# Second norm: which engine normalises, which adds, and in what order GpSimd works

## The reference

```
xn = layernorm(x)
x  = x + linear_attention(xn) + nested_attention(xn)
```

```
q, k = elu(xn @ Wq.T + bq) + 1, elu(xn @ Wk.T + bk) + 1      # linear attention
z    = layernorm(xn) * norm_w + norm_b                       # nested attention
```

## Time and profile before

| | |
|---|---|
| median of 3 runs | 4818.39 us (4813.27 to 4819.5) |
| the profiled execution: time, span | 4783.38 us, 4781.6 us |
| second norm, from its first weight load to the next phase's first load | 2499.4 to 2800.5 us of the span |
| busy in the span: PE, DVE, ACT, POOL | 4446.1, 3305.4, 1912.6, 1037.3 us |

### The profile page before, as it was taken

The page is one execution under the profiler, slowest core; times in us unless marked ns, Lnnn a source line. Parts: engine busy times, 40 slices in busy tenths (PEclk is TensorE's granted clock), DMA queues, the critical chain, the costliest instruction groups (busy, mean ns, idle before and its releaser), DMA issues. The chain is left out here.

```text
span 4781.6 us, 154458 instructions
## 1 busy us (share of the span) xinstructions
PE 4446.1 (93%) x64527; PEld 2868.5 (60%) x64527; DVE 3305.4 (69%) x5496; ACT 1912.6 (40%) x2685; POOL 1037.3 (22%) x1042
## 2 busy tenths in 40 slices
PE   5999699999999999999987879999999999999998
PEld 3444499889889888987655634444444444444443
DVE  5899755555555555554338977878787878787877
ACT  2888311111111111111233426656565656565654
POOL 1000143344334333432007760000000000000000
PEclk9999899999999999999998969999999999999999
DMA  3544411111111111111233440000000000000000
GB/s 121 169 129 126 135 50 53 54 46 51 52 54 50 53 53 47 50 53 58 74 120 105 111 106 9 9 13 9 13 9 13 9 13 9 13 9 13 9 13 9
DMA packets 261647, 250.25 MB, mean 52 GB/s; under 512 B 51712, under 2 KB 230016, under 8 KB 260256
## 3 DMA queue, kind: packets, MB, share of 16 engines
q1 hardware_dynamic: 240528, 209.39, 14.6%
q0 software_dynamic: 6144, 16.79, 1.1%
q10 hardware_dynamic: 14352, 14.55, 0.9%
HBM read 135.27 MB, written 105.38 MB: 50 GB/s over the span
## 5 line engine op out<-in xcount | busy, mean ns | idle before, releaser
L2201 DVE TENSOR_REDUCE part_max<-p_m 128x1 f32<-128x512 f32 x2118 | 1363.2, 685 | 380.8 <-PE p_m L2043 373.3
L2183 ACT ACTIVATE prob<-p_s 128x1024 f32<-128x1024 f32 x1024 | 1047.6, 1023 | 751.0 <-PE p_s L2107 748.9
L2062 PE MATMUL p_o<-prob,v_one 128*64 128x512 f32 x4096 | 1055.1, 593 | 5.2 <-ACT prob L2183 1.8
L2043 PE MATMUL p_m<-keys,queries 96*64 96x512 f16 x4236 | 661.4, 387 | 28.0 <-DMA keys<-parts_d 20.4
L2107 PE MATMUL p_s<-queries,keys 97*64 97x512 f16 x4096 | 618.9, 380 | 0.0
L2107 PEld LDWEIGHTS p_s<-queries,keys 97*64 97x64 f16 x4096 | 228.1, 109 | 599.3 <-issue 593.8
L2043 PEld LDWEIGHTS p_m<-keys,queries 96*64 96x64 f16 x4236 | 238.6, 108 | 311.2 <-DVE part_max L2201 56.4
L2011 POOL TENSOR_TENSOR attn<-o_num,o_inv 32x512 f32<-32x512 f32 x64 | 81.0, 1266 | 1459.5 <-DVE o_inv L2220 1453.1
L833 PE MATMUL pd_pre<-inv,step 64*64 64x64 f32 x10240 | 374.4, 219 | 17.9 <-issue 15.4
L2062 PEld LDWEIGHTS p_o<-prob,v_one 128*64 128x64 f32 x4096 | 287.5, 136 | 164.3 <-issue 15.8
L833 PEld LDWEIGHTS pd_pre<-inv,step 64*64 64x64 f32 x10240 | 342.7, 135 | 46.0 <-issue 45.7
(11 more groups left out here) (245 smaller groups left out, 6701.5 us busy)
## 6 DMA issues: line engine op xcount, KB each, us to landing
q_d<-conv_q SPq DMA_DIRECT2D x16, 1024.0 KB, 5.1
v_d<-conv_v SPq DMA_DIRECT2D x16, 1024.0 KB, 5.1
k_d<-conv_k SPq DMA_DIRECT2D x16, 1024.0 KB, 6.5
sums<-sums_d SPq DMA_DIRECT2D x128, 128.0 KB, 2.9
k_t<-k_d SPq DMA_DIRECT2D x32, 512.0 KB, 4.6
q_t<-q_d SPq DMA_DIRECT2D x32, 512.0 KB, 3.4
v_t<-v_d SPq DMA_DIRECT2D x32, 512.0 KB, 3.3
slots_d<-zero ACTq DMA_DIRECT2D x1, 10112.0 KB, 31.2
```

The source lines that it names most:

```text
L2043: last = te.matmul(p_m[k % 2][x * HALF:(x + 1) * HALF, :], queries[0:ROW, p, hh, at:at + HALF], keys[0:ROW, 2 * p + hh, kb * BLK:(kb + 1) ...
L2062: product = te.matmul(p_o[64 * hh:64 * hh + VW, :], g.v_one[:, j, p, hh:hh + 2, :].rearrange("p a d -> p (a d)"), prob[:, j % 2, hh, :], s ...
L2183: a.activation(prob[:, j % 2], p_s[j % 2][:], ACT.Exp, scale=SCORE_SCALE).then_inc(exp_d, 1)
L2201: v.tensor_reduce(part_max[:, hh * SUB + sub, kb:kb + 1], p_m[k % 2][:], AX.X, ALU.max).then_inc(red_d, 1)
```

## The change

Four things change, all in `phase_second_norm`. Both normalisations go from VectorE to ScalarE, as an activation `Identity` with scale `rstd` and bias `shift`, which GpSimd's `root` makes as -mean * rstd in one more instruction. `add_base` and `query_features` go from GpSimd to VectorE. GpSimd's step becomes `root(a, 0)`, `fetch(s + 1)`, `root(a, 1)`, `remainders(d)`. ScalarE's step becomes `normed(a)`, `key_exp(c)`, `low(d)`, `query_exp(c)`, `keep_turned(b)`, `nested(a)`, `high(c)`; VectorE's becomes `residual(a)`, `sums(d)`, `keys_values(c)`, `normed(a)` (the statistics alone), `queries(c)`, `add_base(a)`, `values(c)`, `query_features(c)`.

```diff
+    shift = sb("s_shift", [P, 2, 2])
...
-        def root(a, n, mv_d, ve_d, rs_d, used_d):
+        def root(a, n, mv_d, ve_d, rs_d, sh_d, used_d):
...
             po.tensor_tensor(rstd[:, r, n:n + 1], var_eps[:, r, n:n + 1], g.minus_half[:], ALU.pow).then_inc(rs_d, 1)
-
-        def add_base(a):
-            pool.wait_ge(base_out[a.r], a.uses * 16)
-            pool.wait_ge(xn1_d, a.t + 1)
-            po.tensor_tensor(base[:, a.r, :], x1[:, a.r, :], xn1[:, a.r, :], ALU.add).then_inc(base_d, 1)
-
-        def query_features(c):
-            pool.wait_ge(q_out[c.r], c.uses * 16)
-            pool.wait_ge(qmax_d, c.t * KC + KC)
-            pool.wait_ge(qexp_d, c.t + 1)
-            po.tensor_tensor(q_feat[:, c.r], q_max[:, c.r], q_min[:, c.r], ALU.add).then_inc(qf_d, 1)
+            pool.wait_ge(rs_d, a.t + 1)
+            po.tensor_scalar(shift[:, r, n:n + 1], mean_var[:, r, n, 0:1], rstd[:, r, n:n + 1], -1.0, ALU.mult, ALU.mult).then_inc(sh_d, 1)
...
         for s in range(NT + 3):
-            a, c, d = (Tile(t, t % 2, t // 2) if 0 <= t < NT else None for t in (s, s - 2, s - 3))
+            a, d = (Tile(t, t % 2, t // 2) if 0 <= t < NT else None for t in (s, s - 3))
+            if a is not None:
+                root(a, 0, mv1_d, ve1_d, rs1_d, sh1_d, xn1_d)
             if s + 1 < NT:
                 fetch(s + 1)
             if a is not None:
-                root(a, 0, mv1_d, ve1_d, rs1_d, xn1_d)
+                root(a, 1, mv2_d, ve2_d, rs2_d, sh2_d, z_d)
             if d is not None:
                 remainders(d)
-            if a is not None:
-                root(a, 1, mv2_d, ve2_d, rs2_d, z_d)
-                add_base(a)
-            if c is not None:
-                query_features(c)
...
     # ScalarE
+        def normed(a):
+            t, r = a.t, a.r
+            act.wait_ge(xnt_d, a.free)
+            act.wait_ge(base_d, a.free)
+            wait_apart(act, g, (sh1_d, t + 1))
+            a_.activation(xn1[:, r, :], x1[:, r, :], ACT.Identity, bias=shift[:, r, 0:1], scale=rstd[:, r, 0:1]).then_inc(xn1_d, 1)
+
+        def nested(a):
+            t, r = a.t, a.r
+            act.wait_ge(zt_d, a.free)
+            wait_apart(act, g, (sh2_d, t + 1))
+            a_.activation(z[:, r, :], xn1[:, r, :], ACT.Identity, bias=shift[:, r, 1:2], scale=rstd[:, r, 1:2]).then_inc(z_d, 1)
...
         def one(ahead, a, b, c, d):
+            if a is not None:
+                normed(a)
             if c is not None:
                 key_exp(c)
             if d is not None:
@@ -1721,6 +1725,8 @@
                 query_exp(c)
             if b is not None:
                 keep_turned(b)
+            if a is not None:
+                nested(a)
             if c is not None:
                 high(c)
...
     # VectorE
-            dve.wait_ge(xnt_d, a.free)
-            dve.wait_ge(rs1_d, t + 1)
-            v.tensor_scalar(xn1[:, r, :], x1[:, r, :], mean_var[:, r, 0, 0:1], rstd[:, r, 0:1], ALU.subtract, ALU.mult).then_inc(xn1_d, 1)
...
-        def nested(a):
-            t, r = a.t, a.r
-            dve.wait_ge(zt_d, a.free)
-            dve.wait_ge(rs2_d, t + 1)
-            v.tensor_scalar(z[:, r, :], xn1[:, r, :], mean_var[:, r, 1, 0:1], rstd[:, r, 1:2], ALU.subtract, ALU.mult).then_inc(z_d, 1)
...
+        def add_base(a):
+            wait_apart(dve, g, (base_out[a.r], a.uses * 16))
+            v.tensor_tensor(base[:, a.r, :], x1[:, a.r, :], xn1[:, a.r, :], ALU.add).then_inc(base_d, 1)
+
+        def query_features(n):
+            dve.wait_ge(q_out[n.r], n.uses * 16)
+            wait_apart(dve, g, (qmax_d, n.t * KC + KC), (qexp_d, n.t + 1))
+            v.tensor_tensor(q_feat[:, n.r], q_max[:, n.r], q_min[:, n.r], ALU.add).then_inc(qf_d, 1)
...
             if a is not None:
-                nested(a)
+                add_base(a)
             if c is not None:
                 values(c)
+                query_features(c)
```

More of the change, by code:

```diff
@@ L1471, in phase_second_norm @@
     routed_in = [sem(f"routed_in{r}") for r in range(2)]
-    half_d, routed_d, x1_d, st1_d, mv1_d, ve1_d, rs1_d, xn1_d, st2_d, mv2_d, ve2_d, rs2_d, z_d = (
-        sem(n) for n in ("half", "routed", "x1", "st1", "mv1", "ve1", "rs1", "xn1", "st2", "mv2", "ve2", "rs2", "z"))
+    half_d, routed_d, x1_d, st1_d, mv1_d, ve1_d, rs1_d, sh1_d, xn1_d, st2_d, mv2_d, ve2_d, rs2_d, sh2_d, z_d = (
+        sem(n) for n in ("half", "routed", "x1", "st1", "mv1", "ve1", "rs1", "sh1", "xn1", "st2", "mv2", "ve2", "rs2", "sh2", "z"))
     xnt_d, xns_d, zt_d, zs_d, kv_d, q_d, qk_d, v_d = (sem(n) for n in ("xnt", "xns", "zt", "zs", "kv", "q", "qk", "v"))
```

## The result

The changed kernel takes 4885.04 us (median of 4 runs, 4875.54 to 4890.02), the kernel before 4815.83 us in the same comparison (4 runs, 4811.53 to 4819.5). The ratio is 1.0146, with a 95% interval of 1.0128 to 1.0165: 1.5% slower, 69 us.

What follows compares the result with a forecast made beforehand. The prediction took VectorE as the bound before and a ring of waits through GpSimd, ScalarE and VectorE after: 28 x 1.93 = 54.0 us, plus 2.4 + 2, makes 58.4 more, 4877 us; range 4868 to 4886.

Steps and rivals of the forecast that it cites:

- the ring is longer: Rival: slower shift or add_base holding up the root; a step of 10.6 to 11.2 us, 4887 to 4901 us; 18 in 100.
- The bound before: Full steps of the kernel before: VectorE sets the 8.37 us, partly by waiting for GpSimd inside xn1.
- what VectorE gives up: VectorE's slots for the two normalisations, xn1 1.35 us and z 0.75 us: 2.10 us a step.
- VectorE's sum: VectorE's list for one step after the change: 8.32 - 2.10 + 0.66 - 0.20 = 6.7 us.
- ScalarE's price: The two normalisations as ScalarE activations of 128x256, taken at 0.42 to 0.6 us; 0.9 us more a step fits.
- the ring: Chain of waits through GpSimd, ScalarE and VectorE back to GpSimd's next root, once a step: 10.20 us, step 10.3.
- first root: Ring term on GpSimd, from the end of mv1 through hand-over and power to shift: 1.41 us.
- gathers: Ring term: two gathers holding GpSimd's queue between first and second root, 2.55 us.
- second root: Ring term on GpSimd behind the gathers: 0.32 + 0.57 + 0.33 = 1.22 us.
- Fill and drain: Outside the full steps: 2.4 us more over three filling steps, 2 us more after the last residual.
- VectorE's relief decides: Rival: the ring is shorter than VectorE's and TensorE's lists; step 7.1 to 7.5 us, some 4788 us; 5 in 100.
- The gathers let the root pass: Rival: gathers hold GpSimd's queue for less than the rows show; step 9.2 us, 4846 us; 10 in 100.

Runs made afterwards that it cites:

- e2: The changed kernel with GpSimd's order of before (gathers, first root, remainder, second root): step 7.76 us, ratio 0.9957 to the kernel before.
- e7: e2 with queries(c) moved ahead of the second statistics on VectorE and the key features behind them: step 6.98 us, ratio 0.9918 to the kernel before.
- e3: The changed kernel with both normalisations back on VectorE: step 10.56 us, ratio 1.0135 to the kernel before.
- e1: The changed kernel with ScalarE's low(d) moved from ahead of query_exp(c) to behind nested(a): step 8.52 us, ratio 1.0015 to the kernel before.
- e8: The changed kernel with two extra copies of 128x512 on ScalarE right behind low(d): step 11.70 us, ratio 1.0208 to the kernel before.
- e4: The kernel before with nothing but GpSimd's new order: step 9.31 us, ratio 1.0055 to the kernel before.
- e10: The changed kernel with GpSimd's remainder between first root and gathers: step 9.97 us, ratio 1.0102 to the kernel before.
- e5: The changed kernel with only the query features back on GpSimd, behind its remainder: step 8.97 us, ratio 1.0043 to the kernel before.

## Why the prediction was right

The direction, the mechanism and its place were right; the size was 58 of 69 us. That the median after, 4885, lies inside the forecast's 4868 to 4886 us is luck: the kernel before came out 2.6 us lower in this comparison (4815.83) than in the runs from which I reckoned (4818.39), and without that it would be 4888. By its step of 10.67 us the result lies outside the forecast's 10.0 to 10.6, at the low end of the rival "the ring is longer". Point by point:

- *The bound before, and what VectorE gives up.* The relief is real. e2 shows it by itself: with the order of before the step is 7.76 us. It did not reach the 6.7 of VectorE's sum because VectorE waits 0.96 us a step for ScalarE's `xn1`; e7 fills most of that wait and comes to 6.98. The collisions of `xn1` are gone.
- *ScalarE's price.* 0.60 us each, at the top of my 0.42 to 0.6. The Trainium skill's budget (ScalarE: Activation LUTs, "Rules for kernel authors"), 0.3 us and 0.83 ns an element, would give an estimate of 0.51 us, but it counts one operand by pointer, the bias, and here scale and bias both are. As foreseen it costs nothing in the ring of after, since the gathers cover it (e3).
- *The ring's terms.* From the rows of after, variance to variance: first root 1.44 us (forecast 1.41), gathers 2.55 (2.55), second root 1.43 (1.22), remainder 1.15 (1.19), cast, exponential and query features 1.45 (1.35), residual 2.50 (2.48). Without the loop's back edge that is 10.5, where 10.2 was counted and 0.1 allowed.
- *One term was mis-sized and one was missing.* The second root is 0.2 us over: in 24 of the 28 full steps its `var_eps` starts just behind `k_feat`, an addition with two inputs in SBUF, and takes 0.41 to 0.48 us; in the other four it starts 0.06 to 0.08 us ahead of `k_feat` and takes 0.23. One step of each kind, from the timelines of GpSimd and VectorE:

```profile
2645.82 0.23 POOL L1573 TENSOR_SCALAR s_var_eps<-s_mean_var 128x1 f32<-128x1 f32 x1
2645.88 0.41 DVE L1792 SCALAR_TENSOR_TENSOR k_feat<-k_pre,k_min 128x256 f32<-128x256 f32 x1
...
2656.46 0.41 DVE L1792 SCALAR_TENSOR_TENSOR k_feat<-k_pre,k_min 128x256 f32<-128x256 f32 x1
2656.54 0.42 POOL L1573 TENSOR_SCALAR s_var_eps<-s_mean_var 128x1 f32<-128x1 f32 x1
```

  I had priced such a collision at 0.1 and put it down to `add_base`. In the groups by line of after, the mean over both roots is 310 ns against the 228 of the earlier trace rows:

```profile
L1573 POOL TENSOR_SCALAR s_var_eps<-s_mean_var 128x1 f32<-128x1 f32 x46 | 14.3, 310 | 95.9 <-DVE s_mean_var L1762 94.3
```

  The missing term is the back edge of VectorE's loop, the jump from its end to its start. The loop's body holds two steps, and ahead of the residual of each of its rounds but the first stand 0.29 to 0.33 us of issue; with a late `var_eps` such a step takes 10.9 us and not 10.53. That is 12 of the 28 full steps, so 12 x 0.37 / 28 = 0.16 us in the mean, and `var_eps` makes 24 x 0.19 / 28 = 0.16. With 0.10 over for the cast and what is behind it: 10.20 + 0.16 + 0.16 + 0.10 = 10.62 of the 10.67 measured; the rest is spread over the other terms. Over the 10.3 of the forecast that is 28 x 0.37 = 10 us, of the 11 by which the whole was short.
- *Fill and drain.* 3.3 and 1.9 us, forecast 2.4 and 2. In the filling steps VectorE waits for the gathers, 2.75 us at tile 1, as foreseen. The 0.9 us over the forecast come from the landing: the second gather is issued at 2556.58 (GpSimd's row) and taken at 2560.01 (VectorE's), 3.4 us later and not the 2.9 that I took, and tile 2 is the same:

```profile
2556.58 1.18 POOL L1564 DMA_INDIRECT share_tile<-y_d,slot  x1 [0.30 <-issue]
...
2560.01 1.00 DVE L1758 SCALAR_TENSOR_TENSOR x<-share_tile,weight,x 128x256 f32<-128x256 f32 x2 [2.75 <-DMA share_tile<-y_d,slot]
```

- *The rivals.* "VectorE's relief decides" needs the ring open, and e2 and e7 show what it is then worth. "The gathers let the root pass" is refuted by the rows of GpSimd: the second root starts at the gather's end in every step. "The ring is longer" is where the truth leaned, 10.67 us, but not for `shift`, which takes 0.27 us.
- *TensorE's clock* fell to 0.84, and it cost nothing that a run could tell: e1 and e8 change ScalarE's queue alone and the step follows, and the step of e4 differs from that of before at the same 0.91, that of e10 from that of after at 0.85 and 0.84. In after TensorE is busy 216.4 of 290 us, 8.0 us a step of 10.67.

## What to carry to other kernels

When work moves between engines that run in order, the sum of each engine's list says who is busy, not how long a step is. Follow the first operation of a step through every queue until it comes back to itself, and add what stands in each queue ahead of the next link; here one cast ahead of one exponential made 2.1 us of a step of 10.7. Transfers issued by a compute engine count in that chain by the time they hold the queue (2.55 us for two gathers); put them where that engine's next input is not ready yet. And a wait taken away can stay as a collision: e1 and e5 lost part of their gain to additions that started beside GpSimd's remainder.

## What was not expected of the hardware

- An operation of GpSimd on 128x1 can be held too: `var_eps` took 0.42 us where it started behind VectorE's `k_feat`, 0.22 to 0.24 in the rest of after. An addition of VectorE's with two inputs in SBUF took 1.19 us beside a GpSimd subtraction of 1.15, and 0.77 beside one of 0.72, where it takes 0.42 alone.
- The gathers' time to landing is no constant: 2.7 to 3.0 us in most steps of the kernel before, but 3.5 to 4.2 for the second gather in e10, where other transfers were issued within a microsecond or so.
- The back edge of VectorE's loop shows as 0.29 to 0.33 us of issue in after, where it stands behind the instruction that waits longest. In the kernel before, whose VectorE never waits, most steps are 8.24 to 8.36 us long.
